# A transformer stack on one core: the first chunk gets its own load semaphore, and its queries are added and split by VectorE in quarters

## What is computed

```python
x = x + jnp.tanh(g_xattn[0]) * _L0_xattn_ref(_layernorm(x, axis=-1), ctx_1024, ...)
x = x + jnp.tanh(g_ffn[0]) * _L0_ffn_ref(_layernorm(x, axis=-1), ...)
# the same pair for layers 1, 2 and 3, with attentions and feed-forward parts of other kinds
```

```python
q = x @ Wq + bq                                  # 16 heads of 8
k = adj @ Wk + bk                                # 4 groups of 8, summed over the groups
v = adj @ Wv + bv
weight = jnp.einsum('bhtd,bgvd->bhtv', q, k) / math.sqrt(D_HEAD)
weight = jax.nn.softmax(weight, axis=-1)
out = jnp.einsum('bhtv,bgvd->bhtd', weight, v)
return out @ Wo + bo
```

## Time and profile before

| what | us |
|---|---|
| median of three runs | 1612.25 |
| lowest and highest of them | 1609.8, 1613.06 |
| the profiled execution | 1613.21 |
| its span | 1611.4 |
| mean granted TensorE clock, share of full | 0.957 |
| TensorE busy in the span | 1416.8 (88%) |
| VectorE busy | 1106.9 (69%) |
| ScalarE busy | 1023.7 (64%) |
| GpSimd busy | 543.4 (34%) |

### The profile page before, as it was taken

How to read it: one execution, slowest core, us unless ns; L and a number is a source line. 1 busy time by engine, 2 the same in 40 slices (tenths; PEclk the granted TensorE clock), 3 DMA queues, 4 the chain that set the end, 5 groups by cost and what they waited for, 6 DMA issues and landing times.

```text
span 1611.4 us, 35134 instructions
## 1 busy us (share of the span) xinstructions
PE 1416.8 (88%) x9978; PEld 1027.8 (64%) x9982; DVE 1106.9 (69%) x3551; ACT 1023.7 (64%) x2947; POOL 543.4 (34%) x627
## 2 busy tenths in 40 slices
PE   2788888998989989899999989999997389999994
PEld 2566655666734446343466666666666289999994
DVE  1788887688767656787467767777777546666665
ACT  2688887554545556222778868788875367777762
POOL 5354466222211221001001413422433635555550
PEclk9899999999989999899999999999997589999998
DMA  8000049700299931000000100100032322222227
GB/s 193 24 8 7 13 69 164 103 0 7 60 165 164 166 49 38 1 1 0 8 8 2 35 19 18 35 22 13 28 125 89 103 60 66 63 67 66 67 58 261
DMA packets 143559, 98.41 MB, mean 61 GB/s; under 512 B 20610, under 2 KB 132652, under 8 KB 142292
## 3 DMA queue, kind: packets, MB, share of 16 engines
q1 hardware_dynamic: 134740, 80.15, 26.1%
q0 software_dynamic: 8704, 16.87, 3.2%
HBM read 43.10 MB, written 54.93 MB: 61 GB/s over the span
## 4 chain that ended last, share of the span: by engine, by line
PE 68%; ACT 11%; DVE 10%; issue 7%; POOL 2%; DMA 1%; SPq 0%; DVEq 0%; ACTq 0%; POOLq 0%
PE bank L983 7%; PE bank L1427 7%; PE bank L1419 7%; PE bank L1271 5%; PE bank L999 4%; PE bank L1034 4%; PE bank L1347 4%; PE bank L924 4%; ACT arena L1460 3%; PE bank L1019 3%; ACT att L1597 3%; PE bank L987 3%; PE bank L1009 3%; ACT att L1462 2%; PE bank L906 2%
## 5 line engine op out<-in xcount | busy, mean ns | idle before, releaser
L1460 ACT ACTIVATE arena<-bank 128x512 f32<-128x512 f32 (+7 forms) x396 | 254.9, 672 | 155.6 <-PE bank L1334 57.9
L1881 ACT ACTIVATE att<-bank,arena 128x128 f32<-128x128 f32 x576 | 165.0, 371 | 73.2 <-PE bank L1419 73.0
L800 POOL DMA_INDIRECT expert_outputs<-arena x144 | 143.6, 997 | 146.6 <-DVE arena L2601 133.2
L1597 ACT ACTIVATE att<-bank,arena 128x128 f32<-128x128 f32 x512 | 180.7, 396 | 15.7 <-DVE arena L2119 14.7
L754 POOL DMA_INDIRECT dispatched_rows<-arena x112 | 115.4, 1030 | 172.0 <-DVE arena L2027 84.6
L602 POOL TENSOR_TENSOR ve<-mv,eps 128x4 f32<-128x4 f32 x64 | 12.9, 202 | 462.8 <-DVE mv L1943 454.9
L1427 PE MATMUL bank<-arena,att 128*128 128x128 f32 x1152 | 153.9, 277 | 1.0 <-ACT att L1881 0.3
L1419 PE MATMUL bank<-xnT,arena 128*128 128x128 f32 x1152 | 154.0, 277 | 0.2 <-ACT xnT L1460 0.2
L1427 PEld LDWEIGHTS bank<-arena,att 128*128 128x128 f32 x1152 | 140.9, 193 | 3.1 <-ACT att L1881 3.1
L1419 PEld LDWEIGHTS bank<-xnT,arena 128*128 128x128 f32 x1152 | 141.6, 194 | 0.6 <-ACT xnT L1460 0.6
L1597 ACT ACTIVATION_READ_ACCUMULATOR att<-bank,arena 128x1 f32 x512 | 120.9, 236 | 0.0
(11 more groups left out here) (360 smaller groups left out, 3255.1 us busy)
## 6 DMA issues: line engine op xcount, KB each, us to landing
dispatched_rows<-padf SPq DMA_DIRECT2D x16, 2128.5 KB, 34.7
arena<-dispatched_rows SPq DMA_DIRECT2D x144, 64.5 KB
cxT<-in_ctx SPq DMA_DIRECT2D x32, 256.0 KB, 2.8
arena<-in_L_ffn_w SPq DMA_DIRECT2D x8, 1024.0 KB
arena<-expert_outputs SPq DMA_DIRECT2D x8, 1024.0 KB, 13.9
expert_outputs<-arena POOLq DMA_INDIRECT x144
out_x<-x SPq DMA_DIRECT2D x8, 256.0 KB, 4.3
dispatched_rows<-arena POOLq DMA_INDIRECT x112
```

Of the source, the lines that this page charges most:

```text
L800: pl.indirect_dma_start(sent_out, bass.IndirectOffsetOnAxis(xtu3[:, s, P:P + 1], 0), yt3[:, s, :], None, bounds_check=TOP3 * TOKENS - 1, o ...
L1460: copy = lambda o, i: nc.scalar.activation(o, i, ACT.Copy)
L1597: last = nc.scalar.activation(ex3_of(w, side)[:, i, :], bank[side][:, i * P:i * P + P], ACT.Exp, bias=nm3[:, w % 2, h:h + 1], accum_out=su ...
L1881: last = nc.scalar.activation(h3[:, s % 2, k * P:k * P + P], bank[s % 2][:, k * P:k * P + P], ACT.Gelu, bias=b1c3[:, s % 4, k:k + 1])
```

## The change

One semaphore becomes three, and VectorE takes over five instructions of GpSimd for the first chunk, cut into four quarters of one sequence each.

- Chunk 0 of x raises x0_loaded. FIRST_LOADS is now only the weights and biases. Chunk 1 of x, wo0 and the rest of x together raise rest_loaded, which is waited for at 48, that is, all three. The order in which SP starts the transfers is the same.
- VectorE begins with the statistics of chunk 0, then waits for the weights (`weights0`), normalises chunk 0, waits for rest_loaded, does `front` of chunk 1, waits for qraw0 and runs `split_queries` four times.
- PE waits before piece 4 + j for count j + 1 of A0_first_queries.
- GpSimd leaves `split` of chunk 0 after the keys, with a wait on A0_slice and a bare increment.
- The semaphores A0_on_full and A0_oT_full are merged into one, counted twice per tile.

```diff
@@ block.sync @@
-                sp.dma_start(FIRST_LOADS[0][0], FIRST_LOADS[0][1]).then_inc(s_first, 16)
+                sp.dma_start(x[:, 0:CB, :], a["x"][0:CB].rearrange("b t d -> t b d")).then_inc(sem("x0_loaded"), 16)
                 sp.dma_start(context(0), cview[:, 0:CB, :]).then_inc(s_cx[0], 16)
-                for dst, src in FIRST_LOADS[1:]:
+                for dst, src in FIRST_LOADS:
                     sp.dma_start(dst, src).then_inc(s_first, 16)
+                sp.dma_start(x[:, CB:2 * CB, :], a["x"][CB:2 * CB].rearrange("b t d -> t b d")).then_inc(sem("rest_loaded"), 16)
                 sp.dma_start(context(1), cview[:, CB:2 * CB, :]).then_inc(s_cx[1], 16)
-                sp.dma_start(wo0[:, :], a["L0_xattn_Wo"]).then_inc(sem("wo0_loaded"), 16)
-                sp.dma_start(x[:, 2 * CB:B, :], a["x"][2 * CB:B].rearrange("b t d -> t b d")).then_inc(sem("x_loaded"), 16)
+                sp.dma_start(wo0[:, :], a["L0_xattn_Wo"]).then_inc(sem("rest_loaded"), 16)
+                sp.dma_start(x[:, 2 * CB:B, :], a["x"][2 * CB:B].rearrange("b t d -> t b d")).then_inc(sem("rest_loaded"), 16)
@@ GpSimd, split @@
                 pl.tensor_copy(ks0[:, :, PARTS0:2 * PARTS0, :], ks0[:, :, 0:PARTS0, :]).then_inc(sem("A0_split"), 1)
+                if isinstance(c, int) and c == 0:
+                    pl.wait_ge(sem("A0_slice"), 4)
+                    pl.sem_inc(sem("A0_split"), 1)
+                    return
                 pl.wait_ge(sem("A0_raw"), c * 2 + 2)
@@ TensorE, piece @@
-                        pe.wait_ge(sem("A0_split"), c * 2 + 2)
+                        if first:
+                            pe.wait_ge(sem("A0_first_queries"), j + 1)
+                        else:
+                            pe.wait_ge(sem("A0_split"), c * 2 + 2)
@@ ScalarE, body @@
-                            act.wait_ge(sem("A0_on_full"), cc * CB + (j + 1))
+                            act.wait_ge(sem("A0_oT_full"), cc * (2 * CB) + (2 * j + 2))
...
-                            act.wait_ge(sem("A0_oT_full"), cc * CB + (j + 1))
+                            if j or not isinstance(cc, int) or cc:
+                                act.wait_ge(sem("A0_oT_full"), cc * (2 * CB) + (2 * j - 1))
@@ VectorE, heads0 @@
+                def split_queries(j):
+
+                    hs = slice(j * HEADS, (j + 1) * HEADS)
+                    of = lambda t, like: t.unsqueeze(2).to_broadcast(list(like.shape))
+                    first, second, third = qs0[:, hs, 0:3, :], qs0[:, hs, 3:6, :], qs0[:, hs, 6:8, :]
+                    v.tensor_tensor(q0[:, hs, :], qraw0[:, hs, :], bq0[:, hs, :], ALU.add)
+                    step(v.tensor_tensor(first, of(qraw0[:, hs, :], first), of(bq0[:, hs, :], first), ALU.add))
+                    v.tensor_tensor(qrest0[:, hs, :], q0[:, hs, :], qs0[:, hs, 0, :], ALU.subtract)
+                    step(v.tensor_tensor(second, of(q0[:, hs, :], second), first, ALU.subtract))
+                    v.tensor_tensor(third, of(qrest0[:, hs, :], third), second[:, :, 0:2, :], ALU.subtract).then_inc(sem("A0_first_queries"), 1)
...
-                for c in range(2):
-                    for k in range(len(parts)):
-                        front(c, k)
-                dve.wait_ge(sem("x_loaded"), 16)
+                dve.wait_ge(sem("x0_loaded"), 16)
+                for k in range(3):
+                    front(0, k)
+                weights0()
+                for k in range(3, len(parts)):
+                    front(0, k)
+                dve.wait_ge(sem("rest_loaded"), 48)
+                for k in range(len(parts)):
+                    front(1, k)
+                dve.wait_ge(sem("A0_raw"), 2)
+                for j in range(CB):
+                    split_queries(j)
                 body(0, 0, True, True)
```

More of the change, by code:

```diff
@@ L413, in flamingo @@
         FIRST_LOADS = [
-            (x[:, 0:CB, :], a["x"][0:CB].rearrange("b t d -> t b d")),
             (wkv0[:, 0, :], a["L0_xattn_Wk"]), (wkv0[:, 1, :], a["L0_xattn_Wv"]),
             (bk0g[:, :], rows(a["L0_xattn_bk"])), (bv0g[:, :], rows(a["L0_xattn_bv"])), (bq0row[:, :], rows(a["L0_xattn_bq"])),
-            (wq0[:, :], a["L0_xattn_Wq"]), (x[:, CB:2 * CB, :], a["x"][CB:2 * CB].rearrange("b t d -> t b d")),
+            (wq0[:, :], a["L0_xattn_Wq"]),
         ]
@@ L912, in body @@
                             pe.wait_ge(sem("A0_normal"), cc * CB + (j + 1))
-                            nc.tensor.transpose(bank[4 + j % 2][:, 0:P], on0[:, j % 2, :], ident[:, :]).then_inc(sem("A0_on_full"), 1)
+                            nc.tensor.transpose(bank[4 + j % 2][:, 0:P], on0[:, j % 2, :], ident[:, :]).then_inc(sem("A0_oT_full"), 1)
                         mine = slices_at(w) if more else []
@@ L952, in heads0 @@
                     piece(0, 0, s, first=True)
-                pe.wait_ge(sem("wo0_loaded"), 16)
+                pe.wait_ge(sem("rest_loaded"), 48)
                 body(0, 0, True, True)
@@ L1556, in heads0 @@
                 act.sem_inc(sem("A0_oT"), 2)
-                act.sem_inc(sem("A0_oT_full"), 1)
                 for s in range(kA):
@@ L1905, in _, with weights0 @@
             dve.sem_inc(s_xdone, 1)
-            dve.wait_ge(s_first, 16 * n_first)
-            dve.wait_ge(s_const, 1)
-            for t, b in enumerate((bk0g, bv0g)):
-                v.tensor_reduce(wkvs0[:, t * D0:t * D0 + D0], wkv0[:, t, :].rearrange("p (g d) -> p d g", g=4), AX, ALU.add)
-                v.tensor_reduce(bkv0[:, t * D0:t * D0 + D0], b[:, :].rearrange("p (g d) -> p d g", g=4), AX, ALU.add)
-            step(v.tensor_scalar(bq0[:, :, :].rearrange("p (j h) d -> p j (h d)", j=CB), bq0row[:, :].unsqueeze(1).to_broadcast([P, CB, P]),
-                                 float(D0) ** -0.5, None, ALU.mult))
+            def weights0():
+                dve.wait_ge(s_first, 16 * n_first)
+                for t, b in enumerate((bk0g, bv0g)):
+                    v.tensor_reduce(wkvs0[:, t * D0:t * D0 + D0], wkv0[:, t, :].rearrange("p (g d) -> p d g", g=4), AX, ALU.add)
+                    v.tensor_reduce(bkv0[:, t * D0:t * D0 + D0], b[:, :].rearrange("p (g d) -> p d g", g=4), AX, ALU.add)
+                step(v.tensor_scalar(bq0[:, :, :].rearrange("p (j h) d -> p j (h d)", j=CB), bq0row[:, :].unsqueeze(1).to_broadcast([P, CB, P]),
+                                     float(D0) ** -0.5, None, ALU.mult))
             def setup():
@@ L2048, in normal @@
                 def normal(c, j):
-                    dve.wait_ge(sem("A0_oT_full"), c * CB + (j + 2))
+                    dve.wait_ge(sem("A0_oT_full"), c * (2 * CB) + (2 * j + 1))
                     o = bank[4 + j % 2][:, :].rearrange("p (i q r) -> p q i r", i=HQ, r=ROWS0)
```

## The result

The changed kernel took 1603.37 us in the median of six runs (1601.52 to 1606.32), and the kernel before 1611.03 in six runs beside it (1608.48 to 1613.06). The ratio is 0.9956, with a 95% interval of 0.9942 to 0.9971: 4.7 to 9.3 us faster, 7.7 by the two medians, where 5.2 was forecast.

The account below looks back on a forecast made before the run. TensorE bounds most of the kernel, but GpSimd's 11.1 us query split stands alone at the start. First scores 5.4 us earlier less 0.2 gives 5.2: 1612.25 to 1607.05, rounded to 1607.0; own range 1605 to 1609, wide range 1603.0 to 1611.0.

Parts of the forecast that it names:

- rival (b): TensorE reaches its higher rate sooner, shortening its chain from 36.96 to 44 us by 2.8: gain 8.0, 1604.2; chance 0.12.
- Landings: Start transfers, unchanged: chunk 0 of x lands at 3.7 us, wq at 8.65, the rest of x at 16.6.
- Part 2: VectorE's wait for the rest of x opens at 16.6 us; quarters begin at 20.5, losing 4.4 of the early gain.
- Part 1: Chunk 0's early start on VectorE: weights end at 9.7, normalisation 4.2 us earlier, queries ready at 16.1 instead of 20.33.
- Part 3, quarters: Chunk 0's query split on VectorE: 2.0 us per quarter, 8.0 for four, where GpSimd took 11.1.
- Part 3, beside GpSimd: VectorE's quarters beside GpSimd's keys, 20.5 to 22.1 us: contention costs 0 to 1.6 us, taken at 0.8.
- Part 4: After the last quarter only the last sequence's transposes and copy remain, 2.25 us: first scores at 31.5, 5.4 earlier.
- Part 5: After first scores: merged semaphores' register instructions in ScalarE's loop cost 0 to 1.2 us, taken 0.2; gain lasts.
- (a): VectorE splits queries no faster than GpSimd, 2.8 us a quarter, costing 3.2 more: gain 2.0, 1610.2; chance 0.10.
- (c): TensorE stays at its lower level through the first body, costing about 9 us: 3.8 slower, 1616; chance 0.06.
- (d): The rest of x lands later, at 20 us instead of 16.6, delaying all behind it: gain 1.8, 1610.4; chance 0.07.

Follow-up runs that it names:

- keys-first run: The changed kernel, but VectorE waits for GpSimd's keys before its first quarter; ratio 0.9968 to the kernel before, median 1623.48 us beside 1627.67.
- one-piece kernel: The changed kernel, but VectorE splits the queries of all four sequences in one go; ratio 0.9976 to the kernel before, median 1625.13 us beside 1629.54.
- the quarters alone: The changed kernel with the early start undone and the rest of x waited for only after the quarters; ratio 0.9962 to the kernel before, median 1624.04 us.
- the semaphores alone: The changed kernel with the query split back on GpSimd in one piece; ratio 1.0013 to the kernel before, median 1630.84 us beside 1629.54.
- second reordering: Chunk 0 normalised before the weights, on the changed kernel with chunk 1's own semaphore; without filler ratio 0.9925 to the kernel before, median 1616.78 us.

## Why the prediction held, step by step

The median of 1603.37 is 3.6 us below the forecast of 1607.0. It lies outside the forecast's own range, 1605 to 1609, and only just inside the wide one, 1603.0 to 1611.0. Of the 3.6, 1.2 are the kernel before, whose six runs have a median of 1611.03 where the first three had 1612.25; 1.2 come from the sum, and the rest is later than stage A3 or noise. By its number the result is nearest to rival (b), a gain of 8.0; the steps below show that (b)'s mechanism was not what gave it.

- **Landings.** Part 2's gate was put at 16.6 from the trace of before. It was 16.2 in the changed kernel (9.7 after the issue instead of 10.1) and 16.6 to 17.1 in the other runs. Right, with a scatter of a few tenths that goes straight into the first scores.
- **Part 1.** Expected: weights ended by wq at 8.7, piece 0 at 11.0, queries at 16.1. Measured 9.2, 11.37, 16.50: wq landed 4.9 after its issue instead of 4.4. As forecast nothing of it reached the scores, because VectorE was held by the rest of x; the run without the early start (0.06) and the one with chunk 1's own semaphore (3.5 us) show both sides.
- **Part 2.** GpSimd's power behind the same wait put the keys at 18.97 (19.4 forecast), ready at 22.54, and cost nothing: the first quarter was done at 22.25, and piece 4 did stand behind piece 3 until 23.00, but TensorE had 0.4 to 0.9 of slack before each of the later pieces. With the split on GpSimd the wait cost 1.7, half of it by a later landing.
- **Part 3, quarters.** 2.0 was taken. The quarters start at 20.07, 22.17, 24.32 and 26.25, and the last ends at 28.25. The third, beside nothing of GpSimd's, took 1.93; the first two hold the 0.4 below. Without it the four took 7.8 instead of 8.0. By form, L2054 took 549 ns in the mean of its four, L2057 424 and L2055 292, where 0.553, 0.423 and 0.292 us had been worked out from rows 7.
- **Part 3, beside GpSimd.** 0.8 was taken as the middle of 0 to 1.6; it was 0.4 (0.17 at one L2056 and 0.23 at one L2053, shown with the keys-first run). This is the term that was sized worst. The rule of the Trainium skill, page "SBUF — State Buffer", section "Who interferes with whom", that such a pair exclude each other, is borne out: in the one-piece kernel GpSimd's 0.25 became 2.43 behind VectorE's 0.68 and 1.75. That the one which starts later waits is not what this trace shows: GpSimd's had begun at 20.46, before VectorE's second (21.04), and ended behind it all the same. What the prediction drew from it, up to the whole overlap on VectorE's side, was too much: the loser was mostly GpSimd, whose instructions ended later, and VectorE was caught only twice.
- **Part 4.** The tail was 2.34 from the last quarter's end at 28.25 to 30.59; 2.25 forecast.
- **Part 5.** The register instructions were put at 0.2. The kernel with the merge alone can't decide it by its time, since the interval of 0.9985 to 1.0010 is wider than the term. In the traces A0 from the first scores to its last score group is 0.3 longer with the merge (238.26, and 238.24 changed, against 237.91), and the quarters alone, which have it too, show nothing (237.83). So it is 0.3 us at the most. The gain stood to the end of A3, 6.1 us, as forecast. The 1.5 us more in the last stage can't be put down to the change: that stage's matmuls (first of L1419 to last of L1453, in the kernels' own numbering) last 312.2 before and 310.9 changed, and 312.8 to 317.0 in the twelve runs on other chips, whose programs are the same there.

So the sum had 5.4 at the first scores and 6.4 came, 1.0 more: 0.4 from the landing, 0.4 from the contention, 0.2 from the quarters, less 0.1 in the tail and some rounding. The mechanism was right, and each of these errors was small; that they all but one lay on the same side is chance. Of the rivals, (a) and (c) did not come, (d) came by tenths, the other way in this trace and against the kernel in the later ones, and (b) did not: the level rose during the transposes at 37.43 (1.34 us, between 1.91 at the lower level and 1.11), some 7 us after the first scores, as before (43.7). In two other kernels, the semaphores alone and VectorE in one piece, (b)'s condition did come, without filler: the first score group took 0.60. But the level was down again by the next piece 1 (1.89), and from the first scores to the second group of transposes it saved at most some tenths (9.98 us, against 9.95 to 10.8 elsewhere), where (b) had put 1.9 to 3.2.

## What to carry to other kernels

A wait that is made earlier for one chunk is worth nothing when the next in-order wait on the same engine holds what hangs on it: look for the first later wait that names more than its own data (here the rest of x where chunk 1 was enough, 3.5 us). Where a serial piece of work at the start has nothing beside it, move it to the engine that does it fastest before cutting it up; on GpSimd, with a fixed cost of 0.19 us per instruction, cutting into four gave nothing back. When two engines hold each other up as here, short instructions on the critical one lose little and let the other through.

## What the runs showed of the hardware

- A GpSimd instruction and VectorE instructions with two SBUF inputs did not overlap in their work: 0.25 became 2.43 us beside two of 0.68 and 1.75. VectorE can be the one that waits: its 0.55 became 0.75 where GpSimd's copy had started 0.2 before (the quarters alone, L2054 at 20.53). The profile counts the time held as part of the instruction.
- The granted clock that the profile shows before its first recorded change of level is not what TensorE ran at. In the kernel before, every stretch up to 44 us reads 1.00 while the transposes took 313 ns against 220 later, that is the lower level, 1.2 GHz; in the runs with filler, where the level changes early, the same durations stand beside a grant of 0.50 (piece 1 of chunk 1 took 1.89 in the kernel before and 1.89 at 38.83 with filler in it). Durations of equal matmuls are the safer reading there.
- The higher level was lost soon after the filler in front of the first body. With filler up to 9.0 us and work from 9.9, the matmuls were at the lower level by 11.7 (2.06 for piece 2); with filler up to 11.8 and nothing until 15.0, piece 0 still began at the higher one (0.87).
- Behind chunk 0's attention the clock fell once or twice (mean grant 0.89 or 0.84 from 56 to 88 us) in kernels whose work there is the same; with one fall instead of two, A0 from the first scores on was 1.5 us shorter in the mean.
- Filling TensorE's gaps with work nobody reads, together with the whole change and the two reorderings, took 16.6 us off the kernel before. The kernel with filler and chunk 1's own semaphore, without the second reordering, measured the same (ratios 0.9887 and 0.9883); either is the one to keep.
